# Three graph layers: gathers and edge loads by group of 256 edges, with slots that look up their group through packed register words

## The chip, the core and the metric

The kernel runs on one core of a Trainium2 chip. The metric is the time of one execution on the device in microseconds (us). Engines: PE (TensorE, matmuls and their weight loads), DVE (VectorE), ACT (ScalarE), POOL (GpSimd) and SP (SyncE, which issues DMAs and waits). ps is PSUM; "arena" is one large tensor in SBUF, which holds nearly everything.

## The reference

3125 nodes with 64 features, 100000 edges sorted by destination, each with an attribute of 64 and one of 32 numbers. Four blocks follow each other, each with a layer norm and relu ahead and a residual behind. The first, three layers of graph attention, takes most of the kernel and is all that the change touches:

```python
q = x @ Wq + bq
k = x @ Wk + bk
v = x @ Wv + bv
e = edge_attr @ We
kj = k[src] + e
alpha = jnp.sum(q[dst] * kj, axis=-1) / jnp.sqrt(jnp.float32(D))
...
msg = (v[src] + e) * w[:, None]                 # w: softmax of alpha over the edges of a destination
agg = jax.ops.segment_sum(msg, dst, num_segments=N)
return agg + x @ Ws + bs
```

The other three blocks (ten steps of propagation, one convolution, one more attention) run behind the three layers on an adjacency matrix of edge counts, which the layers build on the side.

## The kernel before

**Slots.** Destinations are split into 25 blocks of 128 nodes. Edges are sorted, so a slot takes a group of 256 edges (BT = 2 rows of 128) and the part of it that falls into one block. Where a group spans a block's border it appears in two slots: 391 groups (NG) make 415 slots (NBAT). In a setup phase (lines 256 to 533) DVE finds for each slot its group (CI) and block (BI), and the first rows of both are gathered by POOL; SP copies them as rows of words (crow, brow, flag_row) to the partitions from which the engines read them into registers.

**A layer (conv, line 534).** For each slot j:
- POOL waits until the ring slot is free (slot_free, counter bmm), and issues two indirect gathers of 128 node rows each into RING (line 617), whose addresses are constants: `(BT * j) % R_SLOTS`. The ring has 110 rows, 55 slots (RBAT).
- SP waits for the same counter and loads the 256 edge attributes (line 635) from an address that comes from a register: every five slots (REGS) row_values (line 91) loads five words of crow by a TENSOR_LOAD, which the trace shows at line 93.
- ACT makes the one-hot matrix of the slot's destinations (one_hot_rows, lines 668 and 671). PE multiplies it with the block's queries (expand, line 751), block by register.
- DVE waits for the gathers, the load and PE, multiplies with the ring row and sums (product, line 882, a tensor_tensor_reduce, with an accumulator read behind it): alpha for each edge.
- A window is 45 slots (WIN_BATCHES: eight of 45, then 30, 15, 10). After it a softmax over the window is made. DVE then makes, slot by slot, the one-hot matrix with the weights (weighted, line 913, in the last layer also line 916), PE sums the messages (aggregate, line 762, in the last layer also line 766) and counts up bmm, and DVE adds the result to its block (add, line 926), block by register.
- Aggregation of window w-1 and products of window w take turns in one loop, so a ring slot is held from its load until about 45 slots after its product.
- On the side, layers 0 and 1 count sources (sources, count_sources), and all layers build and store edge counts (key_hots, window_counts, copy_counts, store_counts), with registers from flag_row on PE and w4row on ACT, 17 words at a time.

PE runs one expand ahead of the product (`pe.wait_ge(s["pr"], j - 1)` against two buffers UPS). POOL does nothing but gathers in the loop.

```python
for j in range(NBAT):
    slot_free(pool, j)
    for t in range(BT * j, BT * j + BT):
        pool.indirect_dma_start(
            out=RING[:, t % R_SLOTS, XO:XO + XG], out_offset=None, in_=table[:, :],
            in_offset=bass.IndirectOffsetOnAxis(ap=IDX[:, t:t + 1], axis=0)).then_inc(got[j % LEAD], 16)
```

## Time and profile before

| what | value |
|---|---|
| median of 3 runs | 5699.45 us (5696.77 to 5702.19) |
| profiled execution, its own time | 5748.89 us |
| its span, first to last instruction | 5747.1 us |
| mean granted TensorE clock | 0.768 |
| PE / PE weight loads / DVE / ACT / POOL busy | 64 / 53 / 58 / 29 / 44% |
| gathers: line 617 | 2490, of 830 in each layer |
| first gather of layers 0, 1, 2 | 96.2, 1620, 3152.3 us |

The page gives busy times and groups; the trace behind it gives single instructions, waits, and busy times in any stretch. A time is read from the span's start. "idle before, releaser" is the time that an engine sat idle before an instruction and what ended the wait by the profile's semaphore events; "issue" means that it waited for nothing that the profile shows. Where a wait has several semaphores, the last one is named. Sequencer instructions (TENSOR_LOAD, FUSED_REGOPS, waits) don't count as busy; they are marked with a q behind the engine.

### The profile page before, as it was taken

How to read it: one execution, taken by the hardware profiler on the slowest of the kernel's cores; microseconds unless marked ns; L12 is line 12 of the kernel's file. 1: busy time of each engine (PE TensorE's matmuls, PEld its weight loads, DVE VectorE, ACT ScalarE, POOL GpSimd, SP SyncE). 2: the span in 40 equal slices, each digit the busy share in tenths (PEclk: the TensorE clock that was granted, in tenths of full speed). 3: DMA queues.
4: the chain of work that ended last, by engine and by line, in shares of the span. 5: the costliest groups of instructions: out<-in, count | busy, mean ns of one | idle time of the engine just before them, and what ended most of it. 6: DMA issues, size and time to landing. Idle time of an engine off the chain costs nothing. (4 is left out here: it accounts for less than half of the span.)

```text
span 5747.1 us, 88386 instructions
## 1 busy us (share of the span) xinstructions
PE 3660.3 (64%) x23403; PEld 3067.1 (53%) x23403; DVE 3353.9 (58%) x14028; ACT 1690.6 (29%) x3539; POOL 2501.2 (44%) x2592
## 2 busy tenths in 40 slices
PE   2266666666625666666656167777777749999566
PEld 2255554444523555444445156666666649999322
DVE  5166666665624666666657066666666644335699
ACT  0143334443203333344422043333332220000266
POOL 5446665566261655656560635665655220000000
PEclk9977777787755777788777587777776759999688
DMA  2223333333122333334331233333333140000000
GB/s 64 54 76 83 83 89 98 96 101 91 50 52 56 83 82 82 94 98 103 97 87 38 51 82 81 82 82 81 82 81 76 41 162 2 2 2 2 1 3 4
DMA packets 576829, 384.10 MB, mean 67 GB/s; under 512 B 421913, under 2 KB 498833, under 8 KB 576343
## 3 DMA queue, kind: packets, MB, share of 16 engines
q1 hardware_dynamic: 373463, 151.17, 10.3%
q10 hardware_dynamic: 121536, 142.57, 8.0%
q0 software_dynamic: 81344, 84.68, 7.9%
q8 instruction: 207, 3.39, 0.2%
q14 instruction: 279, 2.29, 0.1%
HBM read 312.87 MB, written 65.24 MB: 66 GB/s over the span
## 5 line engine op out<-in xcount | busy, mean ns | idle before, releaser
L617 POOL DMA_INDIRECT arena<-node_table,arena x1660 | 1597.9, 963 | 1233.4 <-PE ps L762 538.1
L762 PE MATMUL ps<-arena 128*128 128x129 f32 x4980 | 1068.3, 351 | 355.9 <-DVE arena L916 124.1
L762 PEld LDWEIGHTS ps<-arena 128*128 128x128 f32 x4980 | 897.6, 253 | 462.7 <-issue 160.7
L882 DVE CUSTOM_DVE_ANT_0 arena<-ps,arena 128x129 f32<-128x129 f32 x2490 | 621.7, 286 | 833.4 <-PE ps L751 334.4
L913 DVE TENSOR_SCALAR arena<-arena 128x128 f32<-128x128 uint16 x2490 | 883.8, 360 | 384.0 <-DMA arena<-in_attr 110.4
L617 POOL DMA_INDIRECT arena<-last_node_table,arena x830 | 795.1, 958 | 596.1 <-PE ps L766 251.0
L751 PE MATMUL ps<-arena 128*128 x2496 | 542.0, 354 | 192.2 <-issue 139.4
L751 PE MATMUL ps<-arena,e 128*128 x2484 | 553.8, 362 | 103.9 <-issue 58.4
L788 PE MATMUL ps<-stage,al 128*128 128x400 bf16 x1190 | 396.2, 425 | 349.7 <-issue 249.9
L751 PEld LDWEIGHTS ps<-arena 128*128 128x128 f32 x2496 | 462.3, 251 | 261.7 <-issue 247.6
L1202 PE MATMUL ps<-arena 128*128 128x192 bf16 x6875 | 587.0, 247 | 13.2 <-issue 7.2
L1202 PEld LDWEIGHTS ps<-arena 128*128 128x128 bf16 x6875 | 584.6, 98 | 15.3 <-issue 12.8
L751 PEld LDWEIGHTS ps<-arena,e 128*128 128x128 f32 x2484 | 473.9, 258 | 170.0 <-issue 158.3
L680 ACT ACTIVATE al<-ps 128x400 bf16<-128x400 f32 x397 | 198.8, 501 | 1086.4 <-DMA arena<-in_attr 450.7
L926 DVE TENSOR_TENSOR arena<-arena,ps 128x129 f32 (+1 forms) x1245 | 364.5, 293 | 157.7 <-issue 81.9
L668 ACT ACTIVATE arena<-arena 128x256 f32<-128x256 bf16 x624 | 314.2, 504 | 396.7 <-issue 116.1
L668 ACT ACTIVATE e<-arena 128x256 f32<-128x256 bf16 x621 | 311.7, 502 | 279.8 <-issue 135.4
L902 DVE TENSOR_SCALAR stage<-arena 128x400 bf16<-128x400 uint16 x1190 | 340.4, 327 | 0.0
L788 PEld LDWEIGHTS ps<-stage,al 128*128 128x128 bf16 x1190 | 115.9, 120 | 386.6 <-issue 343.8
L916 DVE TENSOR_SCALAR arena<-arena 128x128 f32<-128x128 uint16 x830 | 307.1, 370 | 0.1
L766 PEld LDWEIGHTS ps<-arena 128*128 128x128 f32 x1660 | 306.5, 259 | 0.0
L766 PE MATMUL ps<-arena 128*128 128x32 f32 x1660 | 291.1, 306 | 0.0
(340 smaller groups left out, 4014.9 us busy)
## 6 DMA issues: line engine op xcount, KB each, us to landing
arena<-in_attr SPq DMA_DIRECT2D x1245, 96.0 KB
arena<-slot_rows ACTq DMA_DIRECT2D x249, 320.0 KB
edge_counts<-al ACTq DMA_DIRECT2D x397, 100.0 KB
arena<-node_table,arena POOLq DMA_INDIRECT x1660
edge_counts<-stage ACTq DMA_DIRECT2D x198, 100.0 KB
arena<-last_node_table,arena POOLq DMA_INDIRECT x830
arena<-edge_counts SPq DMA_DIRECT2D x24, 500.0 KB
stage<-edge_counts SPq DMA_DIRECT2D x16, 500.0 KB
```

Source lines behind the costliest of these rows:

```text
L617: pool.indirect_dma_start(out=RING[:, t % R_SLOTS, XO:XO + XG], out_offset=None, in_=table[:, :], in_offset=bass.IndirectOffsetOnAxis(ap=I ...
L668: act.activation(o, ROWB[r % 2][:, (j % 5) * BT * P:(j % 5 + 1) * BT * P], ACT.Square, bias=pid1, scale=-1.0)\
L751: ins = pe.matmul(UPS[j % 2][:, q * AB:(q + 1) * AB], OHT[j % 6][:, q * P:(q + 1) * P], U[:, bass.ds(b, 1), :].rearrange("p a b -> p (a b) ...
L762: ins = pe.matmul(BPS[j % 2][:, 0:AB], WOH[j % 2][:, q], RING[:, r + q, D32:D32 + AB], start=q == 0, stop=q == BT - 1)
L766: ins = pe.matmul(BPS[j % 2][:, AB:CW], WOD[j % 2][:, q], RING[:, r + q, 0:D32], start=q == 0, stop=q == BT - 1)
L788: ins = pe.matmul(WPS, LOH[k % 3][:, q], KOH[k % 3][q], start=q == 0, stop=t == 0 and q == G4 - 1)
L882: ins = dve.tensor_tensor_reduce(out=PR[j % 3][:, q], in0=UPS[j % 2][:, q * AB:(q + 1) * AB], in1=RING[:, r + q, D32:D32 + AB], scale=1.0, ...
L902: ins = dve.tensor_scalar(KOH[k % 3][q], iota1[:, 0:NB * WIN], KEY4[:, adj0 + k, q:q + 1], None, ALU.is_equal)
L913: ins = dve.tensor_scalar(WOH[j % 2][:, q], iota1[:, 0:P], DZT[:, t:t + 1], PT[w % 2][:, c:c + 1], ALU.is_equal, ALU.mult)
L916: ins = dve.tensor_scalar(WOD[j % 2][:, q], iota1[:, 0:P], DZT[:, t:t + 1], RING[:, t % R_SLOTS, RW - 1:RW], ALU.is_equal, ALU.mult)
L926: dve.tensor_tensor(to, to, BPS[j % 2], ALU.add).then_inc(s["add"], 1)
L1202: last = pe.matmul(ps[:, o + 256 * c:o + 256 * c + 3 * D], adj3[:, sx, bass.ds((d0 + c) * P, P)], g3[:, sx].rearrange("p a b -> p (a b)"), ...
```

## The change

- Gathers and loads go by group (391) and not by slot (415). The ring holds 55 groups; the place of a gather and of a load is a constant, and the load's address in memory too.
- A slot finds its group's place in the ring by a register: ring_row holds for every four slots (REGS = 4) one word with four places of 6 bits and one word with the number of groups that must have landed. The blocks are packed five bits each in brow, the windows of the counts eight bits each in w4row, the flags one bit each in flag_row. word_value loads a word; field shifts and masks.
- SP loads one word of free_row for each group, waits until PE has aggregated the slots that used the old group, counts up `free`, issues the load, and reports the group that lies four (LAG) back: it waits for its gathers and its load and counts up `landed`. POOL waits for `free`, DVE for `landed` against a value from a register.
- The product becomes a scalar_tensor_tensor with accumulated sum, with the ring row at a register's address; PE's aggregation and, in the last layer, DVE's line 916 take their ring rows from registers too.
- In the setup phase the gathers of source indices by slot and their transposition fall away (the gathers take them from src_t as it is loaded), the packing is added, and POOL gathers the first 24 groups (EARLY) of layer 0 there.

```diff
-LEAD = RBAT
-REGS = 5
+EARLY, LOADS, LAG = 24, 8, 4
+REGS = 4
+NREG = -(-T // REGS)
...
-def row_values(nc, eng, row, at, n, top):
+def word_value(nc, eng, row, at):
+
+    return word_values(nc, eng, row, at, 1)[0]
+
+
+def word_values(nc, eng, row, at, n):
     return nc.values_load_multi_w_load_instructions(
-        row[0:1, at:at + n], engines=[eng], min_val=0, max_val=top,
-        skip_runtime_bounds_check_because="the rows hold chunks, blocks and windows of slots, which are in range for any edges")[1]
+        row[0:1, at:at + n], engines=[eng], min_val=0, max_val=(1 << 24) - 1,
+        skip_runtime_bounds_check_because="the words hold fields of 24 bits together")[1]
+
+
+def field(nc, word, at, bits, top):
+
+    v = (word >> at) & ((1 << bits) - 1) if at else word & ((1 << bits) - 1)
+    return nc.s_assert_within(v, 0, top, skip_runtime_bounds_check_because="the fields hold groups, blocks and windows of slots, in range for any edges")
 def share(n, k, of):
...
+        RING = V(layer_mem, R_SLOTS, RW)
+        RINGS = V(layer_mem, RBAT, BT, RW)
+
+        def gather(pool, i, table, n):
+
+            for t in range(BT * i, BT * i + BT):
+                pool.indirect_dma_start(
+                    out=RING[:, t % R_SLOTS, XO:XO + n], out_offset=None, in_=table[:, :],
+                    in_offset=bass.IndirectOffsetOnAxis(ap=IDX[:, t:t + 1], axis=0)).then_inc(got[i % RBAT], 16)
+
...
-                for fr, to in ((dst_d, DG), (src_d, SG)):
-                    for w in range(NWIN):
-                        pool.indirect_dma_start(
-                            out=to[0:WIN_N[w], w], out_offset=None, in_=fr.rearrange("(g e) -> g e", e=P),
-                            in_offset=bass.IndirectOffsetOnAxis(ap=GI[0:WIN_N[w], w:w + 1], axis=0)).then_inc(rec, 16)
+                for w in range(NWIN):
+                    pool.indirect_dma_start(
+                        out=DG[0:WIN_N[w], w], out_offset=None, in_=dst_d.rearrange("(g e) -> g e", e=P),
+                        in_offset=bass.IndirectOffsetOnAxis(ap=GI[0:WIN_N[w], w:w + 1], axis=0)).then_inc(rec, 16)
...
+                pool.wait_ge(s["lds"], 16)
+                pool.wait_ge(s["xs"], 16)
+                for i in range(EARLY):
+                    gather(pool, i, xt_t, D)
...
+                def pack(to, values, per, bits):
+
+                    n = values.shape[1]
+                    full, words = n // per, -(-n // per)
+                    part = PK[:, 0:words]
+                    if words > full:
+                        st.link(dve.memset(part, 0.0))
+                    for k in range(per):
+                        v = values[:, k::per]
+                        if k:
+                            st.link(dve.scalar_tensor_tensor(part[:, 0:v.shape[1]], v, float(1 << bits * k), part[:, 0:v.shape[1]],
+                                                             ALU.mult, ALU.add))
+                        else:
+                            st.link(dve.tensor_copy(part[:, 0:v.shape[1]], v))
+                    st.link(dve.tensor_copy(to[:, 0:words], part))
+
...
+                dve.tensor_scalar(FQ, FS[0:1, :], 1.0 / BT, None, ALU.mult)
+                st.link(dve.tensor_scalar(QI, CI, float(-(-65536 // RBAT)), None, ALU.mult))
+                st.link(dve.tensor_single_scalar(QI, QI, 16, ALU.logical_shift_right))
+                st.link(dve.scalar_tensor_tensor(WH[:, 0:T], QI, float(-RBAT), CI, ALU.mult, ALU.add))
+                pack(RI[:, 0::2], WH[:, 0:T], REGS, 6)
+                st.link(dve.tensor_scalar(WH[:, 0:NREG], CI[:, 0::REGS], 1.0, None, ALU.add))
+                for k in range(1, REGS):
+                    n = CI[:, k::REGS].shape[1]
+                    st.link(dve.tensor_tensor(PK[:, 0:n], CI[:, k::REGS], CI[:, 0::REGS][:, 0:n], ALU.subtract))
+                    st.link(dve.scalar_tensor_tensor(WH[:, 0:n], PK[:, 0:n], float(1 << 7 + 2 * k), WH[:, 0:n], ALU.mult, ALU.add))
+                st.link(dve.tensor_copy(RI[:, 1:2 * NREG:2], WH[:, 0:NREG]))
...
-                def slot_free(eng, j):
-
-                    if j >= RBAT:
-                        eng.wait_ge(s["bmm"], j - RBAT + 1)
                 @block.gpsimd
                 def _(pool):
                     st = Steps(pool, s["pst"])
-                    for j in range(NBAT):
-                        slot_free(pool, j)
-                        for t in range(BT * j, BT * j + BT):
-                            pool.indirect_dma_start(
-                                out=RING[:, t % R_SLOTS, XO:XO + XG], out_offset=None, in_=table[:, :],
-                                in_offset=bass.IndirectOffsetOnAxis(ap=IDX[:, t:t + 1], axis=0)).then_inc(got[j % LEAD], 16)
+                    for i in range(EARLY if l == 0 else 0, NG):
+                        if i >= RBAT:
+                            pool.wait_ge(s["free"], i - RBAT + 1)
+                        gather(pool, i, table, XG)
                     pool.wait_ge(s["nd"], 1)
                     pool.wait_ge(s["uc"], 5)
                     for i in range(5):
...
-                    for j in range(NBAT):
-                        if j % REGS == 0:
-                            gs = row_values(nc, ET.SP, crow, j, REGS, NG - 1)
-                        slot_free(sp, j)
-                        r = (BT * j) % R_SLOTS
-                        sp.dma_start(RING[:, r:r + BT, 0:XO], at_v[bass.ds(gs[j % REGS], 1), :, :, :].rearrange("o p q f -> (o p) q f"))\
-                            .then_inc(eld[j % LEAD], 16)
+                    def report(i):
+
+                        sp.wait_ge(got[i % RBAT], 16 * BT * (l * len(range(i % RBAT, NG, RBAT)) + i // RBAT + 1))
+                        sp.wait_ge(eld[i % LOADS], 16 * (i // LOADS + 1))
+                        sp.sem_inc(s["landed"], 1)
+
+                    for i in range(NG):
+                        if i >= RBAT:
+                            sp.wait_ge(s["bmm"], word_value(nc, ET.SP, free_row, i - RBAT + 1) & 1023)
+                            sp.sem_inc(s["free"], 1)
+                        r = (BT * i) % R_SLOTS
+                        sp.dma_start(RING[:, r:r + BT, 0:XO], at_v[i]).then_inc(eld[i % LOADS], 16)
+                        if i >= LAG:
+                            report(i - LAG)
+                    for i in range(NG - LAG, NG):
+                        report(i)
...
+                        if j % REGS == 0:
+                            rings[0] = word_value(nc, ET.PE, ring_row, j // REGS * 2)
                         pe.wait_ge(s["woh"], j + 1)
                         if j >= 2:
                             pe.wait_ge(s["add"], j - 1 + window_of(j - 2))
-                        r = (BT * j) % R_SLOTS
+                        r = field(nc, rings[0], 6 * (j % REGS), 6, RBAT - 1)
                         for q in range(BT):
-                            ins = pe.matmul(BPS[j % 2][:, 0:AB], WOH[j % 2][:, q], RING[:, r + q, D32:D32 + AB],
+                            ins = pe.matmul(BPS[j % 2][:, 0:AB], WOH[j % 2][:, q],
+                                            RINGS[:, bass.ds(r, 1), q, D32:D32 + AB].rearrange("p o f -> p (o f)"),
                                             start=q == 0, stop=q == BT - 1)
                         if last:
                             for q in range(BT):
-                                ins = pe.matmul(BPS[j % 2][:, AB:CW], WOD[j % 2][:, q], RING[:, r + q, 0:D32],
+                                ins = pe.matmul(BPS[j % 2][:, AB:CW], WOD[j % 2][:, q],
+                                                RINGS[:, bass.ds(r, 1), q, 0:D32].rearrange("p o f -> p (o f)"),
                                                 start=q == 0, stop=q == BT - 1)
...
                     def product(j):
-                        dve.wait_ge(got[j % LEAD], 16 * BT * (l * len(range(j % LEAD, NBAT, LEAD)) + j // LEAD + 1))
-                        dve.wait_ge(eld[j % LEAD], 16 * (j // LEAD + 1))
+                        if j % REGS == 0:
+                            regs[1], regs[2] = word_values(nc, ET.DVE, ring_row, j // REGS * 2, 2)
+                        k, done = j % REGS, regs[2] & 511
+                        dve.wait_ge(s["landed"], done + ((regs[2] >> (7 + 2 * k)) & 3) if k else done)
                         dve.wait_ge(s["pu"], j + 1)
                         if j >= 3:
                             dve.wait_ge(s["pr"], j - 2)
-                        r, w = (BT * j) % R_SLOTS, window_of(j)
+                        w = window_of(j)
                         for q in range(BT):
                             c = BT * j + q - WIN_T0[w]
-                            ins = dve.tensor_tensor_reduce(out=PR[j % 3][:, q], in0=UPS[j % 2][:, q * AB:(q + 1) * AB],
-                                                           in1=RING[:, r + q, D32:D32 + AB], scale=1.0, scalar=0.0,
-                                                           op0=ALU.mult, op1=ALU.add, accum_out=AL[w % 2][:, c:c + 1])
+                            row = RINGS[:, bass.ds(field(nc, regs[1], 6 * (j % REGS), 6, RBAT - 1), 1), q, D32:D32 + AB].rearrange("p o f -> p (o f)")
+                            ins = dve.scalar_tensor_tensor(PR[j % 3][:, q], UPS[j % 2][:, q * AB:(q + 1) * AB], 1.0, row, ALU.mult, ALU.mult, accum_out=AL[w % 2][:, c:c + 1])
                         ins.then_inc(s["pr"], 1)
                     def sources(j):
...
                     def weighted(j, q):
...
+                        if last and q == 0 and j % REGS == 0:
+                            regs[3] = word_value(nc, ET.DVE, ring_row, j // REGS * 2)
...
-                            ins = dve.tensor_scalar(WOD[j % 2][:, q], iota1[:, 0:P], DZT[:, t:t + 1],
-                                                    RING[:, t % R_SLOTS, RW - 1:RW], ALU.is_equal, ALU.mult)
+                            scale = RINGS[:, bass.ds(field(nc, regs[3], 6 * (j % REGS), 6, RBAT - 1), 1), q, RW - 1:RW].rearrange("p o f -> p (o f)")
+                            ins = dve.tensor_scalar(WOD[j % 2][:, q], iota1[:, 0:P], DZT[:, t:t + 1], scale, ALU.is_equal, ALU.mult)
```

## Rows read from the trace of the kernel before

**Rows 1.** Of the page's section 1: engine, busy us, share of span, instructions

```profile
PE 3660.3 (64%) x23403; PEld 3067.1 (53%) x23403; DVE 3353.9 (58%) x14028; ACT 1690.6 (29%) x3539; POOL 2501.2 (44%) x2592
```

**Rows 2.** Windows of line 617: stretch, length, POOL busy (count), clock, DMA share, GB/s

```profile
622.30:766.15 143.85, 87.54 (x90) 0.71 0.33 83
...
3656.30:3799.50 143.20, 86.42 (x90) 0.68 0.35 83
96.00:235.00 139.00, 104.03 (x110) 1.00 0.27 61
```

**Rows 3.** Timeline: start, duration, engine, line, operation, count, idle before and releaser

```profile
808.61 1.21 PE L751 MATMUL ps<-arena,e 128*128 x4
...
810.48 0.94 POOL L617 DMA_INDIRECT arena<-node_table,arena  x1 [0.30 <-issue]
...
813.05 0.29 DVE L882 CUSTOM_DVE_ANT_0 arena<-ps,arena 128x129 f32<-128x129 f32 x1 [3.26 <-PE ps L751]
813.13 0.95 POOL L617 DMA_INDIRECT arena<-node_table,arena  x1 [1.71 <-PE ps L762]
```

**Rows 4.** Windows, busy of PE, PEld, DVE, ACT, POOL, of two layer starts

```profile
96.00:247.20 151.20, 25.13 (x82) 21.98 (x81) 9.84 (x24) 8.47 (x18) 104.03 (x110) 1.00 0.25 58
...
3152.00:3302.50 150.50, 25.32 (x83) 22.18 (x82) 10.38 (x23) 8.51 (x18) 104.06 (x110) 0.50 0.28 60
```

**Rows 5.** The same view at the start of the second window of layer 0

```profile
337.00:346.00 9.00, 7.18 (x54) 5.82 (x53) 7.92 (x43) 3.93 (x10) 6.20 (x7) 0.97 0.50 141
352.00:361.00 9.00, 6.51 (x33) 5.42 (x33) 5.58 (x31) 3.13 (x8) 5.70 (x6) 0.67 0.29 67
```

**Rows 6.** Windows of line 762 alone in the same stretches: PE, then PEld

```profile
337.00:346.00 9.00, 3.03 (x20) 2.62 (x20) 0.97 0.50 141
352.00:361.00 9.00, 2.78 (x12) 2.42 (x12) 0.67 0.29 67
```

**Rows 7.** Waits of POOL: line, releaser, us in total, times, longest

```profile
POOL arena L617 <- PE ps L762: 538.1, 155, 106.9
...
POOL arena L617 <- PE ps L766: 251.0, 86, 82.1
POOL arena L617 <- DMA arena<-in_attr: 223.7, 148, 2.1
```

**Rows 8.** Timeline of the setup phase

```profile
50.18 0.89 DVE L469 CAST arena<-arena 128x1408 f32<-128x1408 int32 x1 [5.99 <-DMA arena<-in_src,arena]
...
64.38 1.23 POOL L342 DMA_INDIRECT arena<-in_src,arena  x1 [0.30 <-issue]
...
96.18 0.97 POOL L617 DMA_INDIRECT arena<-node_table,arena  x1 [30.58 <-POOLq L88]
```

**Rows 9.** Lines by source: count, min/median/max ns, first and last start

```profile
L751 PEldq FUSED_REGOPS  x1245: 55/55/65, 239.5 to 4606.6; - x178
...
L882 DVE CUSTOM_DVE_ANT_0 arena<-ps,arena x2490: 273/286/296, 247.3 to 4609.5; 128x129 f32<-128x129 f32 x192
...
L926 DVE TENSOR_TENSOR arena<-arena,ps x1245: 270/283/325, 338.6 to 4637.2; 128x129 f32 x119, 128x161 f32 x59
...
L926 DVEq FUSED_REGOPS  x1245: 69/69/75, 338.3 to 4637.0; - x178
```

**Rows 10.** The same view of lines 93 and 635, sequencer instructions

```profile
L93 PEldq TENSOR_LOAD <-arena x286: 585/1238/4555, 238.0 to 4595.5; - x143
L93 DVEq TENSOR_LOAD <-arena x279: 585/1184/1526, 336.8 to 4629.3; - x140
L93 SPq TENSOR_LOAD <-arena x249: 11/1067/1405, 95.5 to 4493.9; - x125
L93 ACTq TENSOR_LOAD <-arena x37: 709/3652/3834, 261.4 to 4336.7; - x37
...
L635 SPq DMA_DIRECT2D arena<-in_attr x1245: 3/373/1399, 97.0 to 4510.8; - x178
```

**Rows 11.** The same view of line 617 in the last layer

```profile
L617 POOL DMA_INDIRECT arena<-last_node_table,arena x830: 940/947/1172, 3152.3 to 4512.2; - x166
```

More of the change, by code:

```diff
@@ L151, in build @@
         ps = ctx.enter_context(nc.psum_tensor("ps", [P, 8 * 512], f32))
-        got = [ctx.enter_context(nc.semaphore(f"gathered{k}")) for k in range(LEAD)]
+        got = [ctx.enter_context(nc.semaphore(f"gathered{k}")) for k in range(RBAT)]
         rec = ctx.enter_context(nc.semaphore("chunks_of_slots"))
@@ L241, in norm_act @@
             act.activation(stat[:, 1], stat[:, 1], ACT.Sqrt).then_inc(s["std"], 1)
-        tmp = Words(layer_mem, LOW + 3225)
-        with phase(nc, "qp ldd ldx ldw lds cst cio cnt gi ms p1 p2 p3 p4 c1 c2 c3 c4 mm mc st var std h row tr key ktr kc wr") as (block, s):
+        tmp = Words(layer_mem + EARLY * BT * RW, LOW + 3225)
+        with phase(nc, "qp ldd ldx ldw lds cst cio cnt gi ms p1 p2 p3 c1 c2 c3 mm mc st var std h row tr key ktr kc xs wr") as (block, s):
             FD = V(tmp.take(NG), NG, dt=i32)
@@ L541, in conv @@
             h_mem = Words(high.at, LOW + HIGH)
-            RING = V(m.take(R_SLOTS * RW), R_SLOTS, RW)
+            m.take(R_SLOTS * RW)
             U = V(m.take(NB * AB), NB, AB)
```

82 lines of the change are left out of this document (35 added, 47 removed).

## The prediction

> **What bounds the kernel now.** I read the page first for shares. No engine is full: DVE is busy 58% of the span and POOL 44% [rows 1]. The profiled execution has a span of 5747.1 us and took 5748.89 us; the runs have a median of 5699.45 us, 49 us less. I make the sum as a difference against the profiled execution and take it off the median, assuming that it carries over.
>
> The kernel's first 4640 us are three graph layers, each with 415 slots of two 128-edge rows; every slot issues two gathers on POOL. A gather holds POOL for 1.25 us: 110 of them, the whole ring, take 139 us, and they stand 0.94 us + 0.30 us apart [rows 2, 3]. Each layer therefore begins with 139 us in which POOL fills the ring. Nothing else gets far in it: from the layer's start to its first product 150 us pass with DVE busy 10 us and PE 25 us, in the first layer as in the last [rows 4].
>
> Then the windows of 45 slots. One lasts 143.85 us in the first layer and 143.20 us in the last [rows 2], although DVE and PE have quite different work there (the last adds a one-hot matrix and two more products of matrices per slot row). The period goes with what is the same in both: 90 gathers, 112.5 us at 1.25 us, and 31.4 us in which POOL issues nothing. The next rows say that this is cause, not chance. At the start of the second window POOL has only begun again: PE runs 20 matmul records of the aggregation (five slots at 4 records) in 9 us and DVE is busy 7.92 us of the 9. A few slots later, with gathers in flight all the time, 12 records (three slots) in 9 us and DVE 5.58 us [rows 5, 6]. So 1.8 us for a slot without the gathers and 3.0 us with them. How they couple is seen in one cycle: PE's expand of 808.61 is over by 809.8, DVE has nothing to do from 809.8 on, and yet its product, which waits for that expand, starts only at 813.05; POOL's last gather ended at 811.42, and it waits until 813.13 [rows 3]. PE's signals come late and in a bunch while gathers are in flight, and pass some 1.5 us after POOL has run dry. POOL waits in this way 389 times, for 538.1, 251.0 and 223.7 us by cause [rows 7] (these hold the long pauses after the fills too). I take a layer between its fill and its last gather to be paced by gathers plus pauses.
>
> **The change part by part.**
>
> *Gathers by group.* 391 groups instead of 415 slots: 48 gathers less in a layer. The fill stays 110 gathers, so all 48 come out of the paced stretch, 720 to 672: 48 x 1.25 = 60 us, 180 us in three layers. Bounds: if the pauses belong to the gather and not to the slot, 48 x 143.85 / 90 = 77 us a layer, 230 us in all; if the slots are not paced by gathers at all, 0. I take 180, since the pauses end with PE's signals, which belong to slots. The loads go down in the same number; they are issued by SP beside all this and cost nothing.
>
> *Early gathers.* In the first layer 24 of the 55 groups of the fill are gathered in the setup phase: 48 x 1.25 = 60 us off the 150 us. They sit on POOL behind the index gathers of the setup, the last of which starts at 64.38 [rows 8]; 11 of those go away (14 us), so the early ones run from about 52 to 112 us, and the phase, after which POOL now starts the fill at 96.18 us, ends at 112 at the earliest: +16 us. If PE's signals are held in the setup as in the fill, the transposes that DVE still needs come only after 112, with some 32 us of work behind them: +48 us. I take +35, net -25 us, with -44 and -12 as ends. The new packing on DVE in the setup (some 45 operations on one partition, at most 0.3 us each, 13 us) partly takes the place of a wait of 5.99 us for the index gathers [rows 8], and lies beside POOL's early gathers; without that cover it would be +7 us.
>
> *Release through SP.* POOL waited for PE's counter itself. Now SP waits for it, against a value loaded per group, counts up "free", and POOL waits for that. Behind SP's wait stand its own load and the reports of "landed". It adds one instruction and one hop to each of POOL's pauses: register instructions take 0.05 to 0.07 us [rows 9], so I take 0.12 us x 389 = +45 us (bounds 0 and 0.25 us each, 97 us). SP's work per group is a word load (1.07 us the median), the load's issue 0.37 us [rows 10] and about five waits and counts at 0.05 us, 1.7 us or so, under POOL's 2.5 us. "Landed" for a group comes only when SP has passed the group four further on. The ring's 55 groups cover 58 slots, aggregation trails the product by about 46, so 12 slots of lead remain and 8 after the lag, 24 us at 3.0: enough.
>
> *Registers on DVE.* Now 279 word loads with a median of 1.18 us, 330 us [rows 10]. After: 104 for the ring (two words) and 104 for the blocks in a layer, and 104 more in the last, 728 in all; with one unit of 0.585 us each 426 us, +100 us on DVE's queue. Each slot gets some 6 more shifts, masks and address sums at 0.069 us [rows 9], 0.41 us x 1245 = 515 us. In the paced stretch DVE idles 3.4 us of 9 [rows 5], and this lies in it. It is not covered in the slots without gathers: about 55 after each fill and 55 after the last gather (in the last layer gathers end at 4512.2 [rows 11], the sums at 4637 [rows 9]). 330 slots; DVE runs ahead in its queue, so of 0.5 us I count 0.15: +50 us (bounds 0 and 165). The product itself changes its instruction: the old one takes 286 ns; the nearest row that reads the same two operands, one of them in PSUM, takes 283 ns [rows 9]. I take 0; its accumulator read stays.
>
> *Registers on PE and ACT.* PE loads words 286 times now, 1.24 us the median and up to 4.6 [rows 10], 355 us by the median and some 400 with the long ones. After, some 223 in a layer, 670 in all, at the fastest row's 0.585 us: 392 us. No difference. The address of the aggregation costs 0.055 us or so each [rows 9], which PE's queue hides. ACT trades 37 loads of mostly 3.65 us for about 200 at 0.71 us: 0.
>
> What a word costs decides this part. The rows do not go by words alone: ACT's loads of up to 17 words took from 0.71 to 3.83 us [rows 10]. The Trainium skill (page "Runtime: NRT & Kernel Launch", section "Instruction fetch mechanics") gives about 200 ns per register, while "DMA: Bandwidth & Descriptors" ("Latency and other measured facts") gives a floor of about 600 ns for such a load. The fastest rows, near 0.58 us for five words, agree with the floor and speak against the other; the sum goes by the rows.
>
> **Sum.** -180 - 25 + 45 + 50 = -110 us. 5748.89 becomes 5639 and the median 5589.
>
> **The rivals.**
>
> *Slower: DVE's queue.* If the register work does not fit under the waits, DVE becomes what paces a slot. Place: the sequencer's work ahead of each product and each add. Price: 0.41 us and 0.08 us more of loads, 0.5 us a slot; if half of it shows in all 1245 slots, +311 us in place of the +50, so 5850. It decides once DVE's busy and sequencer time in the paced stretch passes 3.0 us a slot: it stands at 5.58 / 3 = 1.9 us busy, and its sequencer runs beside that. For it: DVE needs 7.92 of 9 us where nothing holds it. Against: in the paced stretch it idles a third [rows 5]. 0.22.
>
> *No pace by gathers.* The 3.0 us of a slot come from the loop of PE, DVE and ACT under a lower clock; fewer gathers give nothing, the early ones 25 us, the additions take 95 us less what idles: within 10 us of now, 5700. Against it: the equal windows of two layers [rows 2]. 0.09.
>
> *The fill opens up.* SP used to issue 55 loads at once beside the fill; now each waits for a gather four groups back. If those loads, not the gathers, hold PE's signals, the first product needs only the first gathers, and up to half of each fill is won, 3 x 65 us: 5395. Against: in the cycle of 809 to 813 the signals were held by gathers with one load about [rows 3]. 0.07.
>
> *Words pay by number.* With 0.2 us a word PE's loads would fall from 400 us to 135 us. As a mechanism here: PE would stop short for 0.2 instead of about 1.2 us, worth something only in the 330 of 1245 slots without gathers, a quarter of 265, 70 us: 5520. (This is the rule of the Runtime page.) Against: 0.585 us for five words as the fastest [rows 10]. 0.05.
>
> **How the numbers follow.** Forecast 0.57, slower 0.22, no pace 0.09, open fill 0.07, cheap words 0.05. The forecast's own bounds are -230 - 44 = -274 us (5425) and -180 - 12 + 97 + 165 = +70 us, unlikely together; I take 5440 as the low end, which leaves out the open fill, and 5750 as the high end, which leaves out most of the slower case. A measurement of this kernel can tell about 0.2% (11 us) from no change. Faster: 0.57 + 0.07 + 0.05 = 0.69; same 0.09; slower 0.22.
>
> **What would show it.** In the profile after: 782 gathers per layer; a 45-slot window of about 137 us with some 85 gathers, alike in the first and the last layer; pauses of POOL of 1.3 to 1.9 us as before. The setup phase ending between 112 and 145 us, the first product of layer 0 near 225 us, and 149 us after the start of the others. The aggregation's tail up by some 8 us a layer. I am wrong if windows stay near 144 us or grow while DVE's idle share falls (the slower case), if SP's word load stands between a bunch of PE's signals and POOL's next gather, or if a layer's first product comes within 100 us of its start.

## The result and the profile after

The changed kernel takes 5616.84 us, the median of 4 runs (5613.19 to 5624.99), against 5700.82 us: a ratio of 0.9854, with a 95% interval from 0.9837 to 0.9871, or 84 us less. The forecast was 110 us less. The profiled execution took 5613.31 us (span 5611.5 us), near its median; that of before lay 49 us above its own, so the two profiles lie 136 us apart and not 84. Differences between these two profiles are therefore too large, by some 50 us in all. The median of the kernel before was 5701 to 5752 us from chip to chip, and each ratio is to its runs on the same chip; absolute times are compared on one chip where it matters.

The page after, busy times and the gathers' groups (busy us, mean ns | idle before them, main releaser):

```profile
PE 3751.6 (67%) x23392; PEld 3048.8 (54%) x23392; DVE 3445.3 (61%) x14070; ACT 1693.6 (30%) x3539; POOL 2349.9 (42%) x2436
...
L230 POOL DMA_INDIRECT arena<-node_table,arena x1564 | 1512.8, 967 | 1179.4 <-SPq L675 762.5
...
L230 POOL DMA_INDIRECT arena<-last_node_table,arena x782 | 745.0, 953 | 630.9 <-SPq L675 413.8
```

Gathers fell from 2490 to 2346, and POOL waits for SP now and no longer for PE [rows 7]:

```profile
POOL arena L230 <- SPq L675: 1176.2, 512, 101.6
```

The windows of the gathers' line in one 45-slot window of each layer, the ones that answer to [rows 2]:

```profile
577.00:714.60 137.60, 81.38 (x84) 0.72 0.34 83
2042.30:2183.40 141.10, 81.26 (x84) 0.71 0.33 81
3505.30:3648.60 143.30, 80.25 (x84) 0.73 0.34 80
```

84 gathers for 90 in each, but the windows do not shrink alike: 137.6 us in the first layer, 141.1 in the second, and 143.3 in the last, where there is no gain. Over the seven full windows behind the first the means are 144.8, 144.5 and 144.1 us before, and 138.0, 138.7 and 144.8 after. From the end of one layer's sums to the next, the layers took 1582, 1530 and 1524 us, and now 1497, 1468 and 1524. What comes behind the layers went from 1110 to 1122 us. By these two profiles the change won 85 us in the first layer, 62 in the second and nothing in the third, and lost 12 us in a part of the kernel that it doesn't touch: 135 us, where the medians give 84.

Two kernels of the experiments below ran on one chip and correct this: the kernel before with paced loads, which takes the time of the kernel before, and the changed kernel without its early gathers. Their layers took 1573, 1527 and 1522 us against 1547, 1479 and 1535, and what comes behind 1110 against 1123. The mean of the seven windows went from 143.9, 144.7 and 143.9 to 141.0, 140.4 and 146.0 us. So, early gathers apart, the change won 26 us in the first layer and 48 in the second, and lost 13 in the third and 12 behind the layers; with the 40 us or so of the early gathers that comes near the measured 84. In the last layer the windows did not merely stay, they grew by 2 us, which is one of the prediction's own signs of being wrong, met in one layer of three.

The beginnings, from the timeline (start, duration, engine, line, operation, idle before and its releaser). POOL's early gathers, the first of the layer itself, the first product of layer 0, then first gather and first product of layer 1:

```profile
48.43 0.97 POOL L230 DMA_INDIRECT arena<-node_table,arena  x1 [0.30 <-issue]
...
116.75 0.95 POOL L230 DMA_INDIRECT arena<-node_table,arena  x1 [0.30 <-issue]
124.78 0.95 POOL L230 DMA_INDIRECT arena<-node_table,arena  x1 [7.08 <-POOLq L90]
...
219.87 0.29 DVE L934 SCALAR_TENSOR_TENSOR arena<-ps,arena 128x129 f32<-128x129 f32 x1 [2.35 <-PE ps L795]
...
1536.16 0.98 POOL L230 DMA_INDIRECT arena<-node_table,arena  x1 [29.31 <-POOLq L90]
...
1659.72 0.29 DVE L934 SCALAR_TENSOR_TENSOR arena<-ps,arena 128x129 f32<-128x129 f32 x1 [10.79 <-remote]
```

The early gathers run from 48.4 to 117.7 us and the layer goes on at 124.8; the first product comes at 219.9 us, 27 us before that of before (247.3). In layer 1 it comes 123.6 us after the first gather, where it came after some 149 to 151 us in all layers [rows 4]; in the last layer it comes after 130.6 us. The first window then takes longer, so that its end, the place where the next stage can begin, moves from 243 to 233 us after the first gather in layer 1, and from 217 to 209 in the last.

The word loads, which answer to [rows 10]:

```profile
L100 SPq TENSOR_LOAD <-arena x1008: 5/267/722, 216.8 to 4344.6; - x168
L100 DVEq TENSOR_LOAD <-arena x734: 4/530/954, 216.2 to 4485.4; - x184
L100 PEldq TENSOR_LOAD <-arena x661: 13/474/770, 217.6 to 4481.5; - x166
L100 ACTq TENSOR_LOAD <-arena x201: 274/282/473, 228.7 to 4455.0; - x101
```

DVE's group mixes three kinds, which the order of its sequencer's instructions tells apart. The two-word load ahead of every fourth product has a median of 0.747 us, the one-word load of the blocks 0.528 us, the one-word load for the second one-hot matrix 0.318 us. SP, ACT and PE load one word each time: 0.267, 0.282 and 0.474 us. So a word has no single price. The same one-word load of the blocks takes less where its engine has no ring words to load; DVE with the ring's constants (an experiment below):

```profile
L104 DVEq TENSOR_LOAD <-arena x318: 298/304/551, 296.8 to 4389.6; - x159
```

PE's median falls in the same way, from 0.474 to 0.305 us, when its ring words are constants. Why is not shown. The prediction took one unit of 0.585 us for each load: PE's cost 299 us in all where 392 were reckoned, DVE's 402 us where 426 were reckoned.

### The profile page after: what moved, and what is told of

Same layout as the page of the kernel before. It is cut to its first block and busy times, and to the rows that moved or that the text cites. A ratio compares the mean times of both kernels' runs of the same rounds, so it can differ in the third digit from the quotient of the medians.

```text
span 5611.5 us, 110710 instructions
## 1 busy us (share of the span) xinstructions
PE 3751.6 (67%) x23392; PEld 3048.8 (54%) x23392; DVE 3445.3 (61%) x14070; ACT 1693.6 (30%) x3539; POOL 2349.9 (42%) x2436
## 5 line engine op out<-in xcount | busy, mean ns | idle before, releaser
L230 POOL DMA_INDIRECT arena<-node_table,arena x1564 | 1512.8, 967 | 1179.4 <-SPq L675 762.5
L808 PE MATMUL ps<-arena 128*128 x4980 | 1079.9, 353 | 450.7 <-issue 160.4
L808 PEld LDWEIGHTS ps<-arena 128*128 128x128 f32 x4980 | 877.2, 248 | 598.1 <-issue 593.2
L934 DVE SCALAR_TENSOR_TENSOR arena<-ps,arena 128x129 f32<-128x129 f32 x2490 | 632.9, 289 | 774.1 <-issue 305.9
L230 POOL DMA_INDIRECT arena<-last_node_table,arena x782 | 745.0, 953 | 630.9 <-SPq L675 413.8
L965 DVE TENSOR_SCALAR arena<-arena 128x128 f32<-128x128 uint16 x2490 | 878.5, 358 | 162.2 <-PE ps L808 49.3
L795 PE MATMUL ps<-arena 128*128 x2496 | 559.7, 362 | 177.1 <-issue 103.9
L795 PEld LDWEIGHTS ps<-arena 128*128 128x128 f32 x2496 | 454.2, 252 | 273.6 <-issue 269.8
L795 PEld LDWEIGHTS ps<-arena,e 128*128 128x128 f32 x2484 | 446.4, 248 | 197.2 <-issue 193.4
L835 PE MATMUL ps<-stage,al 128*128 128x400 bf16 x1190 | 382.9, 412 | 173.1 <-issue 101.6
L813 PEld LDWEIGHTS ps<-arena 128*128 128x128 f32 x1660 | 309.1, 261 | 0.2 <-issue 0.2
L969 DVE TENSOR_SCALAR arena<-arena 128x128 f32<-128x128 uint16 x830 | 293.2, 353 | 14.8 <-issue 13.1
L813 PE MATMUL ps<-arena 128*128 x1660 | 293.5, 308 | 0.1
```

What stands on the lines that cost most here:

```text
L230: pool.indirect_dma_start(out=RING[:, t % R_SLOTS, XO:XO + n], out_offset=None, in_=table[:, :], in_offset=bass.IndirectOffsetOnAxis(ap=ID ...
L795: ins = pe.matmul(UPS[j % 2][:, q * AB:(q + 1) * AB], OHT[j % 6][:, q * P:(q + 1) * P], U[:, bass.ds(b, 1), :].rearrange("p a b -> p (a b) ...
L808: ins = pe.matmul(BPS[j % 2][:, 0:AB], WOH[j % 2][:, q], RINGS[:, bass.ds(r, 1), q, D32:D32 + AB].rearrange("p o f -> p (o f)"), start=q = ...
L813: ins = pe.matmul(BPS[j % 2][:, AB:CW], WOD[j % 2][:, q], RINGS[:, bass.ds(r, 1), q, 0:D32].rearrange("p o f -> p (o f)"), start=q == 0, s ...
L835: ins = pe.matmul(WPS, LOH[k % 3][:, q], KOH[k % 3][q], start=q == 0, stop=t == 0 and q == G4 - 1)
L934: ins = dve.scalar_tensor_tensor(PR[j % 3][:, q], UPS[j % 2][:, q * AB:(q + 1) * AB], 1.0, row, ALU.mult, ALU.mult, accum_out=AL[w % 2][:, ...
```

## The experiments

### Half of the gathers

```diff
-                        for t in range(BT * j, BT * j + BT):
+                        for t in range(BT * j, BT * j + (BT if j < RBAT else 1)):
...
-dve.wait_ge(got[j % LEAD], 16 * BT * (l * len(range(j % LEAD, NBAT, LEAD)) + j // LEAD + 1))
+dve.wait_ge(got[j % LEAD], 16 * (l * (1 + len(range(j % LEAD, NBAT, LEAD))) + j // LEAD + BT))
```

> The kernel before, with the second of a slot's two gathers left out from slot 55 of each layer on (the rows keep what an earlier slot left in them, so a part of the node values is wrong). If gathers pace the slots: a slot costs one gather of 1.25 us and the loop falls back to its own pace without gathers, 1.8 to 2.0 us a slot, so a window of 45 slots falls from 144 us to 80 to 92 us, 24 windows, about -1250 us, 4450 us in all. If the loop of PE, DVE and ACT sets the 3.0 us of a slot and gathers only go beside it: windows stay near 144 us, 5700 us.

Ratio 0.8348, from 0.8319 to 0.8376: some 950 us less. Windows of 45 slots took 94 to 109 us in most, and 117 to 124 us in the last three of the seven full windows of the first two layers. Three of them, all engines (PE, PEld, DVE, ACT, POOL, clock, DMA share, GB/s):

```profile
529.60:629.70 100.10, 73.14 (x506) 60.38 (x504) 89.08 (x465) 46.51 (x108) 43.74 (x45) 0.89 0.43 104
860.00:977.70 117.70, 80.91 (x487) 64.77 (x486) 88.88 (x447) 58.43 (x133) 46.08 (x45) 0.88 0.43 110
2960.50:3060.50 100.00, 79.32 (x585) 71.73 (x585) 90.00 (x455) 45.47 (x106) 43.91 (x45) 0.91 0.44 103
```

The windows fall by 20 to 50 us for 45 gathers less, 0.45 to 1.1 us for each. So gathers do set the period of 144 us, and "no pace by gathers" is out. The pace that is left, with one gather a slot, is 2.1 to 2.8 us and not 1.8 to 2.0, with a granted clock of 0.9 where it was 0.7. The two come together: PE's busy time in the first layer's window fell from 93.5 to 73.1 us. How much of the gain comes from the clock and how much from signals that are no longer held, this run doesn't separate. Why the last three windows are longer is open too.

### Loads paced in the kernel before

```diff
                         slot_free(sp, j)
+                        if j >= 4:
+                            sp.wait_ge(got[(j - 4) % LEAD], 16 * BT * (l * len(range((j - 4) % LEAD, NBAT, LEAD)) + (j - 4) // LEAD + 1))
```

> The kernel before, with one wait added: SP issues the load of slot j only when the gathers of slot j-4 have landed, as in the changed kernel. Nothing else differs. If the loads issued at once hold up a layer's beginning: the first product comes 125 to 130 us after the layer's first gather and not 150, -20 to -25 us in each layer, -60 to -75 us in all (5630 us), windows stay at 144 us. If the fill is a matter of gathers alone: the first product stays at 150 us, 5700 us.

Ratio 0.9993, from 0.9982 to 1.0003: nothing. The first gather and the first product of layer 1:

```profile
1611.77 0.98 POOL L617 DMA_INDIRECT arena<-node_table,arena  x1 [29.62 <-POOLq L88]
...
1752.23 0.29 DVE L884 CUSTOM_DVE_ANT_0 arena<-ps,arena 128x129 f32<-128x129 f32 x1 [9.99 <-DMA arena<-in_attr]
```

140.5 us for 148.9, and 143 and 141 for 151 and 150 in layers 0 and 2: the first product comes 8 to 9 us earlier, and the first window is 4 to 7 us longer for it (its end moved by 2 to 4 us). Pacing the loads is not what opens the fill, and a first product that comes early is worth little by itself: the end of the first window must be read.

### Without the early gathers

```diff
-EARLY, LOADS, LAG = 24, 8, 4
+EARLY, LOADS, LAG = 0, 8, 4
```

> The changed kernel without the early gathers (EARLY = 0): layer 0 gathers all of its groups itself. By the prediction's step the 24 early groups give 25 us, so 5642 us, and the first product of layer 0 comes 150 us after its first gather. By the rival (the paced loads shorten the beginning of each layer, early gathers or not): first product of layer 0 at 125 to 130 us after its first gather, so that what the early gathers give is between 0 and 10 us, 5620 us.

Ratio 0.9930, from 0.9906 to 0.9953. The changed kernel had 0.9854 and, in a second series on another chip, 0.9862, so the early gathers are worth 39 to 43 us with some 17 us of uncertainty.

```profile
99.03 0.97 POOL L230 DMA_INDIRECT arena<-node_table,arena  x1 [50.93 <-POOLq L90]
...
225.55 0.29 DVE L934 SCALAR_TENSOR_TENSOR arena<-ps,arena 128x129 f32<-128x129 f32 x1 [10.82 <-issue]
```

The first product came 126.5 us after the first gather, as the rival had it, but the gain did not vanish: the first window ends at 331 us and with the early gathers at 301 or 302 us, 30 us. The step's 25 us were about right, and the rival was wrong since it looked at the first product only.

### Ring registers as constants

All ring places, landed counts and freeing slots as constants for these edges. The core of it:

```diff
-                        dve.wait_ge(s["landed"], done + ((regs[2] >> (7 + 2 * k)) & 3) if k else done)
+                        dve.wait_ge(s["landed"], GROUP[j] + 1)
...
-                            row = RINGS[:, bass.ds(field(nc, regs[1], 6 * (j % REGS), 6, RBAT - 1), 1), q, D32:D32 + AB].rearrange("p o f -> p (o f)")
+                            row = RINGS[:, GROUP[j] % RBAT, q, D32:D32 + AB]
...
-                        r = field(nc, rings[0], 6 * (j % REGS), 6, RBAT - 1)
+                        r = GROUP[j] % RBAT
...
-                            sp.wait_ge(s["bmm"], word_value(nc, ET.SP, free_row, i - RBAT + 1) & 1023)
+                            sp.wait_ge(s["bmm"], START[i - RBAT + 1])
```

> The changed kernel, with each slot's ring place, the number of groups that must have landed and the slot that frees a group written in as constants that hold for these edges; only the blocks' registers stay. Nothing is left out of the computation. It prices all register work of the ring on DVE, PE and SP. By the prediction's step: -50 us (5567 us), from the ends of the layers, paced windows unchanged at 138, 139 and 145 us. By the rival that register work costs in the paced windows of the last layer: these fall from 145 to 137 us, -64 us more, near 5500 us. If it was all covered: 5617 us.

Ratio 0.9547, from 0.9526 to 0.9568: about 175 us below the changed kernel, three times the 50 that the prediction gave for all of it. The rival in this expectation had the last layer's windows right (138 us), but its total, some 115 us, is also too low: it left the other two layers' windows as they were.

```profile
568.00:705.50 137.50, 80.87 (x84) 0.72 0.35 83
2005.00:2143.50 138.50, 80.90 (x84) 0.75 0.35 83
3429.20:3567.80 138.60, 80.37 (x84) 0.76 0.36 82
```

The window of the last layer has come down from 143.3 to 138.6 us and now stands beside the other two. The kernel with paced loads ran on the same chip and behaves as the one before, so the two can be compared: its seven windows and the next, of 30 products, took 1149, 1154 and 1151 us in the three layers, and here they take 1089, 1086 and 1096. That is 183 us in all for 144 gathers, 1.27 us for each, near the prediction's 180. It is not a price of gathers alone: the hop through SP and the new product instruction are in these windows too.

The changed kernel without its early gathers ran on this chip as well. The same eight stretches took 1119, 1114 and 1161 us in it, so the ring's registers cost 31, 29 and 65 us there. In the last layer that is more than the 54 us that fewer gathers give.

### The changed kernel again, and constants on one engine at a time

The changed kernel once more, and the edits above on DVE alone and on PE alone.

> The changed kernel itself, once more, on the chip of the three that follow, so that they can be compared with it: ratio 0.985 to the kernel before, windows 138, 139 and 145 us in the three layers.

> The changed kernel with the ring's places and the number of landed groups as constants on DVE alone; PE and SP keep their registers. If it is DVE's queue that pays for registers: nearly all of what constants everywhere gave comes from here, ratio 0.955 to 0.962, and the last layer's paced windows fall from 145 to 137 or 138 us. If it is PE's word loads and addresses: ratio near 0.98 and the last layer's windows stay at 144 to 145 us.

> The changed kernel with the ring's places as constants on PE's aggregation alone; DVE and SP keep their registers. If DVE's queue pays: ratio 0.98 to 0.985, last layer's windows at 144 to 145 us. If PE pays: 0.96 and 138 us.

Ratios on one chip: the changed kernel 0.9862 (0.9842 to 0.9882), constants on DVE 0.9676 (0.9660 to 0.9692), constants on PE 0.9756 (0.9740 to 0.9773). In medians 5620.33, 5517.59 and 5567.27 us: DVE's ring registers cost 103 us and PE's 53. Neither theory had both. Together they are 156 us of the 175 or so for all ring registers; what remains is SP's, or the engines' together, and within the uncertainty of some 20 us. DVE's is the larger part, and only its removal brings the last layer's windows down (mean of seven: 143.9 us, with DVE's constants 138.8, with PE's 143.4). By the profiles, DVE's part is 17, 11 and 39 us in the eight windows of the three layers, and 34 us at the layers' beginnings and ends: two thirds of it lie in the paced stretch, where the prediction had none.

DVE busy in a window, then the register instructions. The kernel before, all engines, first and last layer:

```profile
622.30:766.15 143.85, 93.50 (x506) 76.83 (x504) 91.71 (x464) 46.59 (x108) 87.54 (x90) 0.71 0.33 83
...
3656.30:3799.50 143.20, 110.54 (x585) 101.26 (x585) 92.43 (x455) 45.61 (x106) 86.42 (x90) 0.68 0.35 83
```

The changed one:

```profile
577.00:714.60 137.60, 96.64 (x509) 75.85 (x508) 94.46 (x464) 47.23 (x109) 81.38 (x84) 0.72 0.34 83
...
3505.30:3648.60 143.30, 107.69 (x588) 95.29 (x587) 97.64 (x456) 46.44 (x107) 80.25 (x84) 0.73 0.34 80
```

Constants on DVE, last layer:

```profile
3447.40:3586.20 138.80, 107.06 (x587) 94.22 (x585) 91.80 (x456) 45.83 (x106) 80.30 (x84) 0.73 0.35 82
```

In the last layer's window DVE was busy 92.4 us before, 97.6 after, and 91.8 with constants. Beside that its sequencer's register instructions and word loads, added up from the instructions of the same stretches, take 14 us before and 61 us after (56 and 606 of them); in the first layer's window 45 us after. Register work runs in part beside busy time. Counted without the overlap, DVE does one or the other for 95 us of the last layer's window before, 116 after and 92 with constants; in the first layer for 96 before and 106 after. So 27 us of the last layer's 143 are still free of both, where 49 were before: the windows grew although the idle time was not used up. A likely reason, which no run shows by itself, is that the work stands in the queue ahead of a product or a one-hot matrix for which others wait.

The second part is what one register instruction costs. The changed kernel with gathers in flight, 3505 to 3649 us, count and min/median/max ns:

```profile
L926 DVEq ALU_OP  x111: 4/45/689, 3507.1 to 3648.2; - x111
...
L978 DVEq ALU_OP  x77: 4/45/707, 3510.4 to 3639.0; - x77
...
L978 DVEq FUSED_REGOPS  x44: 5/69/708, 3510.6 to 3639.0; - x44
```

And the same lines behind the last gather, 4364 to 4489 us:

```profile
L926 DVEq ALU_OP  x60: 40/45/53, 4368.7 to 4459.7; - x60
...
L978 DVEq ALU_OP  x90: 40/45/45, 4366.2 to 4486.9; - x90
...
L978 DVEq FUSED_REGOPS  x52: 69/69/69, 4366.3 to 4487.0; - x52
```

The median is the same, but with gathers about single ones take up to 0.7 us; without, none is over 0.07. Over the layers 485 of DVE's 12,770 register instructions (1275 before) took over 0.3 us, 327 us together out of 944. None did where no gather was in flight (218 to 297, 1400 to 1497, 4350 to 4488 us), and none in the kernel before on DVE, or with constants on DVE, in which the same lines have 57 and 75 ns at most. On SP the kernel before had 189 such. So gathers in flight are needed for a long one but are not enough: they flew in those kernels too. PE is alike, with none over 0.3 us in the kernel before or with constants on PE, and 86 in the changed one. What else it takes, the number of instructions perhaps, no run separates, and so it stays open how much of the 103 us is due to the long ones.

### POOL without SP between

Constants as above, and:

```diff
-                            pool.wait_ge(s["free"], i - RBAT + 1)
+                            pool.wait_ge(s["bmm"], START[i - RBAT + 1])
...
-                            sp.sem_inc(s["free"], 1)
```

> The changed kernel with all ring registers as constants, and POOL waiting for PE's count itself, without SP between; SP waits for the same count for its load. Against the same constants with SP between (ratio 0.955). By the prediction's step, 0.12 us for each of some 430 pauses of POOL: another -45 us, ratio 0.947. By its lower bound (the hop is hidden): 0.955. Pauses of POOL after a run of gathers would be 0.1 us shorter in the first case.

Ratio 0.9537, from 0.9521 to 0.9553, against 0.9547 with SP between: 6 us, with some 15 of uncertainty. POOL's waits:

```profile
POOL arena L234 <- PE ps L809: 530.0, 183, 95.5
...
POOL arena L234 <- remote: 258.5, 171, 2.0
POOL arena L234 <- PE ps L814: 247.3, 89, 74.5
```

It waits 443 times here and 435 with SP between. The pauses after a run of four gathers have a median of 1.27 us against 1.36, so a hop of some 0.1 us is there. What it costs stays open: between nothing and about 20 us, since the two kernels ran on different chips. The 45 us of the step are not borne out.

### Two ways on: fewer registers, and a ring that is filled by and by

Fewer registers: DVE waits once in four slots, for the last group of the four.

```diff
                         if j % REGS == 0:
                             regs[1], regs[2] = word_values(nc, ET.DVE, ring_row, j // REGS * 2, 2)
-                        k, done = j % REGS, regs[2] & 511
-                        dve.wait_ge(s["landed"], done + ((regs[2] >> (7 + 2 * k)) & 3) if k else done)
+                            dve.wait_ge(s["landed"], regs[2] & 511)
```

Filling by and by:

```diff
                         if i >= RBAT:
                             pool.wait_ge(s["free"], i - RBAT + 1)
+                        elif i >= max(RAMP, EARLY if l == 0 else 0):
+                            pool.wait_ge(s["pr"], i - RAMP + 1)
```

> The changed kernel with DVE waiting for landed groups once in four slots, for the last group of the four, instead of once a slot: the second word holds that number alone, and about 2.2 of DVE's 9 or so added register instructions a slot fall away; word loads stay as many. If register instructions pay in proportion (constants on DVE gave 106 us for all of them and for 416 loads): 20 to 28 us, ratio 0.981 to 0.982, nearly all in the last layer and in the slots without gathers. If only word loads pay: 0.986. If the slots' lead of some 8 groups was needed: slower than 0.986.

> The changed kernel with POOL held back while it fills the ring: from group 12 on (24 in layer 0) it waits until the product of the slot eleven before it is made. If gathers in flight hold PE's signals, as in the fill of 139 us: PE's beginning and the first product get through after 12 groups, some 50 to 60 us after the layer's first gather, and the first 45 slots go at 3.0 us; the first window ends 185 to 195 us after the start where it ends at 233 now, -40 us a layer (-25 in the last), -100 us in all, ratio 0.968. If the beginning of a layer takes its time whatever POOL does: the first product stays at 124 to 135 us, and the first window grows by what the fill is late, ratio 0.986 to 1.0.

> The two edits before together. If they act in different places (the layer's beginning, and DVE's queue later): the gains add up, 0.963 to 0.965. If either is in the other's shade: as the better of the two.

> Both edits, with 24 groups gathered at once and not 12 (60 us of gathers and not 30 at the start of layers 1 and 2; layer 0 as before). If PE's signals wait for POOL to run dry: first products of layers 1 and 2 come 25 to 30 us later than with 12, their first windows end 10 to 25 us later, ratio 0.003 to 0.008 above the same with 12.

On one chip: fewer registers 0.9817 (0.9788 to 0.9846), filling by and by 0.9724 (0.9694 to 0.9754), both 0.9663 (0.9635 to 0.9692), both with 24 groups 0.9680 (0.9656 to 0.9705). Against the 0.9862 and 0.9854 of the changed kernel the first is 21 to 26 us, as expected but with intervals that touch; on top of the second it is 28 us (5586.98 to 5558.92), with intervals that don't. DVE's register instructions fell from 12,770 to 9971 and those over 0.3 us from 485 to 264. By the profiles of the last two kernels 16 of the 28 us lie in the last layer's eight windows. The second is 74 to 79 us, its mechanism as expected. POOL and then DVE in layer 1 of the kernel with both:

```profile
1532.08 0.98 POOL L231 DMA_INDIRECT arena<-node_table,arena  x1 [29.33 <-POOLq L91]
...
1560.89 0.94 POOL L231 DMA_INDIRECT arena<-node_table,arena  x1 [0.30 <-issue]
1580.26 0.95 POOL L231 DMA_INDIRECT arena<-node_table,arena  x1 [18.43 <-DVE arena L934]
```

```profile
1579.48 0.29 DVE L934 SCALAR_TENSOR_TENSOR arena<-ps,arena 128x129 f32<-128x129 f32 x1 [2.31 <-PE ps L796]
```

POOL stops after 24 gathers, PE and DVE get through their beginning, and the first product comes 47.4 us after the first gather (123.6 in the changed kernel); with 24 groups it comes after 76 us. The first window ends after 188 and 187 us in layers 1 and 2, where it was 233 and 209; with 24 groups after 202 and 193, but the whole is not measurably slower for it. So the late first product is the gathers' doing in the main: the loads are held back with them here, but pacing the loads alone moved it by 8 to 9 us only. The version with both edits, which holds no constants of these edges, beats both kernels: 0.9663.

## Why the prediction was right in its sum, and where its terms were wrong

- *What bounds the kernel* was right. Leaving out 1080 of the 2490 gathers took 950 us, and with constants for the registers the windows stand at 137 to 138 us in all layers, as the prediction had them.
- *Gathers by group*, -180 us: measured -183 us where the register work is out of the way, with the hop through SP in it.
- *Early gathers*, -25: the traces give 30 us at the end of the first window and the ratios 39 to 43. Setup ended at 124.8 us (112 to 145), the first product came at 219.9 (225).
- *Release through SP*, +45: not borne out, 6 us with 15 of uncertainty. The hop of 0.1 us shows in the pauses.
- *Registers on DVE*, +50 with bounds 0 and 165: 103 us. Two parts of the step failed. It counted "some 6 more" register instructions a slot, and there are 9.2 (11,495 in 1245 slots): the unpacking of the landed count takes 2.5 a slot, and with the addresses of the two products it was reckoned too low. And it said that in the paced stretch all this "lies in" DVE's idle third. The third was there in the last layer as well (92.4 us busy of 143.2), and it was not used up, yet two thirds of the 103 us arose in the paced windows, most of it in the last layer, where DVE also reads the ring for its second one-hot matrix. What failed is the inference from an idle share to no cost. For the slots without gathers, the only place where it saw a cost, 34 us stand against its 50.
- *Registers on PE*, 0: 53 us, though its word loads got cheaper (299 us after 411). Loads were counted; of the 4.4 shifts and addresses that the ring adds to a slot on PE's queue one address was named and said to be hidden, and 11 us arise behind the layers (below).
- *The fill opens up*: not by paced loads, which give 8 to 9 us at the first product and nothing in the time. It does open where POOL is held back. The sign given for it, the first product 149 us after the start of the other layers, was wrong for the changed kernel, with 123.6 and 130.6 us; the end of the first window moved by 8 to 10 us only.
- *Words pay by number*: in part. One word takes 0.27 to 0.53 us by engine and place and two take 0.75 us at the median, so the step's unit of 0.585 us was too high for one word and too low for two. The Trainium skill's floor of about 600 ns ("DMA: Bandwidth & Descriptors", "Latency and other measured facts") doesn't agree with one word in 0.27 to 0.53 us; its 200 ns per register ("Runtime: NRT & Kernel Launch", "Instruction fetch mechanics"), which the page gives for loads from HBM, is the nearer, if low by these rows. PE's loads fell by 112 us in all, and the kernel was none the faster for it: PE's part of the change still cost 53 us.
- *The slower rival*, DVE's queue, was the right place. Its price of 0.5 us a slot was too high in the first two layers, and in the last the registers of all engines took more than the gain. Its condition, busy and sequencer time over 3.0 us a slot, is met by the plain sum (3.1 us in the first layer, 3.5 in the last) and not once the overlap is taken off (2.4 and 2.6).
- Not in the sum: with constants everywhere the ends of the three layers together are 16 us shorter and the first windows of layers 1 and 2 together 17 us shorter than with the paced loads. Why is open.

By ratios: constants everywhere are 258 us below the kernel before, and the ring's registers with SP between cost about 175 of it back. The forecast of -110 took a gain of 205 and a price of 95, of which 45 for the hop. That the total came within 28 us is thus in part luck, two errors that cancel: 258 us gained, with the hop already taken off, where 160 were forecast, and 175 us paid for registers where 50 were. Part of the larger gain lies at the layers' beginnings and ends, part is the hop that hardly costs.

## What to carry to other kernels

An idle share is no proof of a cover. DVE idled a third of each window, register work was put beside it, and the windows grew with a fifth still free: only the runs that took the work out gave its price, and they gave another for each stage. Two profiles can differ by chip and run by half of what the change is worth and more (49 us here), so compare stages on one chip. Registers in place of constants are paid per instruction, so count what the unpacking really issues, and replace a wait per item by one per word where the lead allows it. And an engine that runs ahead can hold up all the others: holding POOL back by a count of finished products won 74 to 79 us, nearly as much as the whole change, with two lines.

## What the hardware did that was not expected

- Register instructions on a sequencer take 0.045 or 0.069 us, but in the changed kernel, with gathers in flight, some 4% of DVE's took 0.3 to 1.4 us, mostly 0.7. In the kernel before, gathers in flight too, none of DVE's 1275 did.
- A TENSOR_LOAD of one word takes 0.27 to 0.53 us at the median, of two words 0.75 (DVE). In the kernel before, five words took 0.59 us in every fourth load ahead of a product on DVE and 1.19 us in the others. No run shows why.
- Code that isn't running any more has a price. The ten steps of propagation behind the layers hold no ring register, and yet took 553 us after and 542 before, from their first product of matrices to the last; 543 with constants on PE, 552 with those on DVE alone, 541 with both. DVE's waits for PE there, in the changed kernel and with constants on PE:

```profile
DVE arena L1421 <- PE ps L1252: 302.7, 50, 13.3
```

```profile
DVE arena L1423 <- PE ps L1254: 292.9, 50, 10.5
```

It goes with PE's registers in the layers' code. What carries it over is not shown.
